# Products of queries and projection matrix: from one unrounded product per head to three products of rounded operands in halves of the array, with the queries and the matrix split beforehand

## What is computed

```python
def features(data, proj, is_query):             # data: q or k, 12 heads, 625 x 64
    dash = einsum('bhnd,md->bhnm', data * 64 ** -0.25, proj)   # proj: 266 x 64
    diag = sum(data ** 2, -1) * 0.5 * 64 ** -0.5
    stab = max(dash, -1) if is_query else max(dash)            # per row, or over everything
    return 266 ** -0.5 * (exp(dash - diag - stab) + 1e-4)
q1, k1 = features(q, P, True), features(k, P, False)
kv = einsum('bhnm,bhnd->bhmd', k1, v)
out = einsum('bhnm,bhmd->bhnd', q1, kv) / einsum('bhnm,bhm->bhn', q1, sum(k1, 2))
```

## Time and profile of the kernel before

| | |
|---|---|
| median of 3 runs | 1195.68 us (1194.62 to 1196.69) |
| the profiled execution, its own time | 1196.4 us |
| its span in the trace | 1194.7 us |
| mean granted clock of TensorE | 0.985 of full speed |
| TensorE busy | 1142.5 us, 96% |
| VectorE / ScalarE / GpSimd busy | 762.3 / 657.6 / 450.2 us |
| float32 feature products of the queries (L1704) | 120 instructions, from 204.1 to 285.8 us |

### The profile page before, as it was taken

One profiled execution on the slowest core, in us unless ns is written; L12 is line 12 of the kernel. 1 busy time (PEld: TensorE's weight loads), 2 busy tenths in 40 slices (PEclk: granted clock), 3 DMA queues, 4 the chain that ended last, 5 costly groups with the idle time before them and its releaser, 6 DMA issues.

```text
span 1194.7 us, 20786 instructions
## 1 busy us (share of the span) xinstructions
PE 1142.5 (96%) x6492; PEld 1008.1 (84%) x6493; DVE 762.3 (64%) x1226; ACT 657.6 (55%) x1040; POOL 450.2 (38%) x340
## 2 busy tenths in 40 slices
PE   6989999999999999999999999999999999999985
PEld 5989998888665778989999888888889989998874
DVE  7881454365587466526956865647775896666883
ACT  3222575165400154347686685757876878386963
POOL 1188888788811000542122231203223542122511
PEclk9989999999989999999999999999999999999998
DMA  9030003340300330166687565565785959377933
GB/s 312 18 89 3 2 2 82 113 140 3 87 9 18 103 118 13 28 182 222 212 305 259 211 233 187 176 224 187 285 295 203 367 188 335 83 274 286 351 118 97
DMA packets 63088, 191.71 MB, mean 160 GB/s; under 512 B 14315, under 2 KB 15382, under 8 KB 63044
## 3 DMA queue, kind: packets, MB, share of 16 engines
q1 hardware_dynamic: 51316, 172.86, 39.6%
q0 software_dynamic: 11728, 18.27, 8.9%
HBM read 178.74 MB, written 15.09 MB: 162 GB/s over the span
## 4 chain that ended last, share of the span: by engine, by line
PE 78%; DVE 9%; issue 4%; ACT 4%; DMA 3%; POOL 1%; ACTq 0%; SPq 0%; DVEq 0%; POOLq 0%
PE banks L1939 25%; PE banks L1923 24%; PE banks L1689 3%; PE banks L1704 3%; PE banks L1837 3%; PE banks L1859 3%; PE banks L1672 3%; PE banks L1907 2%; PE banks L1761 2%; PE banks L1739 2%; PE banks L1911 2%; ACT kfeat L1432 2%; DMA out<-ysb,sidx 2%; PE banks L1900 1%; DVE oh L962 1%
## 5 line engine op out<-in xcount | busy, mean ns | idle before, releaser
L730 POOL DMA_INDIRECT edge_dram<-epair,eslot x165 | 219.6, 1331 | 98.9 <-issue 98.9
L520 ACT ACTIVATE w2hi<-w2raw 128x1536 fp32r<-128x1536 f32 x96 | 139.2, 1483 | 95.3 <-DMA w2raw<-in_L_ffn_fc_w 83.7
L794 POOL DMA_INDIRECT out<-ysb,sidx x27 | 84.9, 3143 | 264.8 <-issue 231.0
L533 DVE TENSOR_TENSOR w2lo<-w2raw,w2hi 128x1536 fp32r<-128x1536 f32 x96 | 164.4, 1754 | 25.9 <-ACT w2hi L520 23.8
L1939 PE MATMUL banks<-w2hi,hthi 128*128 128x384 f32 x624 | 161.7, 340 | 0.1
L1939 PE MATMUL banks<-w2hi,htlo 128*128 128x384 f32 x624 | 159.2, 335 | 0.0
L1939 PE MATMUL banks<-w2lo,hthi 128*128 128x384 f32 x624 | 158.9, 335 | 0.0
L520 ACT ACTIVATE w1hi<-w1raw 128x1536 fp32r<-128x1536 f32 x96 | 137.8, 1498 | 27.2 <-DMA w1raw<-in_L_ffn_fc_w 25.9
L1923 PE MATMUL banks<-w1hi,xthi 128*128 128x512 f32 x486 | 139.7, 396 | 2.7 <-POOL w1lo L533 2.7
L533 DVE TENSOR_TENSOR w1lo<-w1raw,w1hi 128x1536 fp32r<-128x1536 f32 x80 | 141.6, 1834 | 0.1
L1923 PE MATMUL banks<-w1lo,xthi 128*128 128x512 f32 x486 | 136.8, 390 | 0.0
(11 more groups left out here) (347 smaller groups left out, 1866.2 us busy)
## 6 DMA issues: line engine op xcount, KB each, us to landing
w1raw<-in_L_ffn_fc_w SPq DMA_DIRECT2D x96, 768.0 KB
w2raw<-in_L_ffn_fc_w SPq DMA_DIRECT2D x96, 768.0 KB, 6.4
xs<-in_x SPq DMA_DIRECT2D x10, 336.0 KB
edge_dram<-epair,eslot POOLq DMA_INDIRECT x165
wg<-in_L_gnn_W SPq DMA_DIRECT2D x1, 2304.0 KB, 12.5
wv<-in_L_mix_W_qkv SPq DMA_DIRECT2D x1, 2304.0 KB, 13.9
wk<-in_L_mix_W_qkv SPq DMA_DIRECT2D x1, 2304.0 KB, 17.8
wq<-in_L_mix_W_qkv SPq DMA_DIRECT2D x1, 2304.0 KB, 12.0
```

The costliest lines, as they stand in the source:

```text
L520: act.activation(unit(w2hi if second else w1hi, second, u), unit(w2raw if second else w1raw, second, u), ACT.Copy).then_inc(w2_hi if secon ...
L533: eng.tensor_tensor(unit(w2lo if second else w1lo, second, u), unit(w2raw if second else w1raw, second, u), unit(w2hi if second else w1hi, ...
L730: pool.indirect_dma_start(out=edge_dram, out_offset=bass.IndirectOffsetOnAxis(ap=eslot[:, k:k + 1], axis=0), in_=epair[:, k, :].bitcast(I3 ...
L794: pool.indirect_dma_start(out=out, out_offset=bass.IndirectOffsetOnAxis(ap=sidx[:, 0:1], axis=0), in_=ysb[:, :], in_offset=None, bounds_ch ...
```

## The change

Queries and matrix are split as other operands are. ScalarE copies `projt` into `projhi` and each tile's queries into `qhi`; the first two of these stand ahead of the last two key exponentials, behind a wait for all squares, the other four after them. VectorE makes `projlo` after the last key features, in place of `projt`, and `qlo` in place of `qt`: tile 0 right after it, the others between the key-value copies. TensorE waits for `projlo` ahead of the key tails. `query_pair` replaces two calls of `project`: it waits for the banks of both heads and for the tile's low part, and then makes three rounds (high x high, high x low, low x high) of one product per head. The keys' products (`ddk`) stay as they are. `projhi` lies where `xs` has its fifth row tile, so that tile's second load moves behind the last transposes.

```diff
--- before.py
+++ after.py
@@ -163,6 +163,8 @@
         hs = at("hs", 89088, [TP, NT, D])
         xn2 = at("xn2", 73728, [TP, NT, D])
         qt = at("qt", 104192, [128, C, N])
+        qlo = at("qlo", 104192, [128, C, N], F32R)
+        qhi = at("qhi", 88832, [128, NT, C, TP], F32R)
         xn2t = at("xn2t", 104448, [128, 2, C, TP])
         kt = at("kt", 119296, [128, C, N])
         q1 = [at("q1a", 119296, [TP, H, M]), at("q1b", 132128, [TP, H, M])]
@@ -274,6 +276,8 @@
         eslot = at("eslot", s0 + 1344, [TP, ET], U32)
         bsplit = small("bsplit", [128, F + D], BF16)
         projt = at("projt", s0, [128, M])
+        projlo = at("projlo", s0, [128, M], F32R)
+        projhi = at("projhi", 198560, [128, M], F32R)
         nbias = at("nbias", s0 + 1472, [TP, 4, 60])
         lnst = at("lnst", s0 + 1472, [TP, NT, 2, 6])
         lnmv = at("lnmv", s0 + 1728, [TP, NT, 2])
@@ -433,7 +437,7 @@
 
         half_hi, half_lo, vones_ok, sq_ok, sq_used, kmax_ok, kbias_ok, kexp_ok, k1_ok = sems(
             "half_hi half_lo vones_ok sq_ok sq_used kmax_ok kbias_ok kexp_ok k1_ok")
-        qbias_ok, q1_ok, q1t_used, bsplit_zero = sems("qbias_ok q1_ok q1t_used bsplit_zero")
+        q_high, q_low, proj_high, proj_low, qbias_ok, q1_ok, q1t_used, bsplit_zero = sems("q_high q_low proj_high proj_low qbias_ok q1_ok q1t_used bsplit_zero")
         gate_pad, shared_rows, shared_ok, xt_zero = sems("gate_pad shared_rows shared_ok xt_zero")
 
         x1_ok, xn2_ok, sc_ok, ex_ok, member_ok, slots_ok, btab_ok = sems(
@@ -606,10 +610,13 @@
             sp.dma_start(bias1_dram.rearrange("g e (j c) -> (e j) g c", j=8), bias_s[:, :, 0:F // 8]).then_inc(st_bias, 16)
             sp.dma_start(bias2_dram.rearrange("g e (j c) -> (e j) g c", j=8), bias_s[:, :, F // 8:]).then_inc(st_bias, 16)
 
-            done(sp, ("sqq", 0))
-            for i in range(NT):
+            def rows_again(i):
                 for a, b in ((0, 112), (112, TP)):
                     sp.dma_start(xs[a:b, i, :], x[TP * i + a:TP * i + b, :]).then_inc(ld_x[i], 16)
+
+            done(sp, ("sqq", 0))
+            for i in range(NT - 1):
+                rows_again(i)
             sp.dma_start(wp[:, :, :], w_proj.rearrange("(c p) n -> p c n", c=C)).then_inc(ld_wp, 16)
 
             fc1_units = fc1_w.rearrange("e (c p) n -> e p c n", c=C)
@@ -630,6 +637,7 @@
             sp.dma_start(bias2[:, 0, :], row(gnn_b).broadcast_to([TP, D])).then_inc(ld_bias, 16)
             sp.dma_start(bias2[:, 1, :], row(b_proj).broadcast_to([TP, D])).then_inc(ld_bias, 16)
             done(sp, ("q1t", 4, H // 2 - 1))
+            rows_again(NT - 1)
             sp.wait_ge(st_offs, 16)
             sp.dma_start(offs[:, :], row(region_dram)[:, 0:ET_TILES]).then_inc(ld_offs, 16)
             for u in range(3):
@@ -1082,6 +1090,18 @@
                 dve.tensor_scalar(q1tail[:, i % 2, heads, :], q1[i % 2][:, heads, MAIN:M], FEAT_EPS, ratio,
                                   ALU.add, ALU.mult).then_inc(q1_ok, 1)
 
+            def query_low(i):
+
+                dve.wait_ge(q_high, i + 1)
+                t = slice(TP * i, TP * i + TP)
+                dve.tensor_tensor(qlo[:, :, t], qt[:, :, t], qhi[:, i, :, :].bitcast(F32), ALU.subtract).then_inc(q_low, 1)
+
+            dve.wait_ge(proj_high, 1)
+            done(dve, ("ddk", NT - 1, H - 2))
+            done(dve, ("ddk", NT - 1, H - 1))
+            dve.tensor_tensor(projlo[:, :], projt[:, :], projhi[:, :].bitcast(F32), ALU.subtract).then_inc(proj_low, 1)
+            dve.wait_ge(sq_ok, 2 * C)
+            query_low(0)
             squares_to(("sqq", 0), 1)
             taken(dve, ("sqq", 0))
             for g in range(2):
@@ -1095,6 +1115,8 @@
                     emptied(dve.tensor_copy(kv[:, h, :, :], ps[:, 0:2 * (HD + 1)].rearrange("p (m d) -> p m d", m=2)), ("kv", h))
                     if h % 2:
                         q_bias(0, h // 2)
+                    if h in (1, 3, 5, 9):
+                        query_low((h + 1) // 2 if h < 9 else NT - 1)
                     if h == 7:
                         q_features(0, 0)
 
@@ -1447,7 +1469,19 @@
             for n in range(2, 10):
                 exp_keys(7 * n - 12, 7 * n - 5)
                 take_columns("q", (n + 2) // 2, (n % 2,))
+            act.wait_ge(sq_ok, 2 * C)
+            act.activation(projhi[:, :], projt[:, :], ACT.Copy).then_inc(proj_high, 1)
+            for o in range(C):
+                for s in range(2):
+                    taken(act, ("q", o, s))
+
+            def query_high(i):
+                act.activation(qhi[:, i, :, :], qt[:, :, TP * i:TP * i + TP], ACT.Copy).then_inc(q_high, 1)
+
+            query_high(0)
             exp_keys(58, H * NT)
+            for i in range(1, NT):
+                query_high(i)
 
             def q_exp(i, p):
                 for h in (2 * p, 2 * p + 1):
@@ -1717,6 +1751,18 @@
                     filled(pe.matmul(ps[0:TP, 0:TP], kmax[0:TP, 0:1].broadcast_to([TP, TP]), ident[0:TP, 0:TP],
                                      start=True, stop=True), ("kmx", 0))
 
+            def query_pair(i, r):
+
+                parts = [(fill(pe, ("ddq", i, h)), HD * (h % 2), h) for h in (2 * r, 2 * r + 1)]
+                pe.wait_ge(q_low, i + 1)
+                for k, (of, w) in enumerate(((qhi, projhi), (qhi, projlo), (qlo, projhi))):
+                    for ps, a, h in parts:
+                        stationary = qlo[a:a + HD, r, TP * i:TP * i + TP] if of is qlo else qhi[a:a + HD, i, r, :]
+                        last = pe.matmul(ps[0:TP, 0:M], stationary, w[a:a + HD, :], start=k == 0, stop=k == 2)
+                        if k == 2:
+                            filled(last, ("ddq", i, h))
+
+            pe.wait_ge(proj_low, 1)
             pe.wait_ge(vones_ok, 1)
             for s in range(2):
                 taken(pe, ("v", NT - 1, s))
@@ -1740,8 +1786,7 @@
                                              vext[:, i, h, :], start=i == 0, stop=i == NT - 1)
                     filled(last, ("kv", h))
                     if h % 2:
-                        project("ddq", qt, 0, h - 1)
-                        project("ddq", qt, 0, h)
+                        query_pair(0, h // 2)
 
 
             def turn_pair(i, p):
@@ -1782,8 +1827,7 @@
                         filled(pe.transpose(ps[0:TAILS, 0:TP], q1tail[:, i % 2, :, :].rearrange("p h m -> p (h m)"),
                                             ident[0:TP, 0:TP]), ("tail", i))
                     for r in AHEAD[p] if i + 1 < NT else ():
-                        project("ddq", qt, i + 1, 2 * r)
-                        project("ddq", qt, i + 1, 2 * r + 1)
+                        query_pair(i + 1, r)
                     attend(i, p)
```

## The result

The changed kernel takes **1206.99 us** (median of 4 runs, 1206.45 to 1209.77), the one before 1195.96 in the same comparison (1194.62 to 1196.69): ratio 1.0101, 95% interval 1.0085 to 1.0117. It is slower, as forecast, but by 11.0 us where I had 5.6, and above the range of 1198.6 to 1205.5. Its profiled execution took 1206.46 us.

What follows compares the result with a forecast made beforehand. TensorE, busy 96% of the span, was taken as the bound, with no slack at the seam behind the key exponentials. +5.25 + 1.75 - 0.46 - 0.9 = +5.6 us gave 1201.3 us, range 1198.6 to 1205.5.

Steps and rivals of the forecast that it cites:

- Seam, (a) to (d): Between query-column products and key-value products: waits for the splits add 5.25 us, the lower clock after TensorE's stop 1.75.
- the place of the wait: TensorE waits for the matrix's low part ahead of all key tails, so eight early tail instructions come behind it: 2.6 us.
- (a): At the seam ScalarE makes two high parts before the last two key exponentials, so the last features come 2.25 us later.
- (b): At the seam VectorE then makes the matrix's low part, 0.44 us, done at 199.8.
- (d): TensorE's idle stop at the seam lowers its clock for 3.5 us of work, half lost: +1.75 us, bounds 0 and 3.4.
- Pairs in tile 0: Six pairs between tile 0's key-value products, where TensorE is the pace, gain 0.46 us in all.
- in a stream: Pairs following each other take 0.375 us each, 0.073 less than now; three pairs take 1.34 us instead of 1.62.
- Rival (1): In the pairs the array's halves take turns, 0.75 us a pair: in all +13.6 us, 1209.3; chance 0.10.
- rival (2): Weight loads set the pairs' pace, 0.54 us a pair: in all +9.0 us, 1204.7; chance 0.12.
- Loop: The 24 pairs in the loop over tiles gain 0.22 us per tile, 0.9 in four; bounds 0 and 2.8.
- rival (4): Not slower: 1.2 GHz stretches near 239, 330 and 346 us vanish and the new stop is free, 1194.5; chance 0.04.
- Moved: Row tile 4's second load goes later at no cost, under 2 us if late; a later TensorE is passed on in full.

Runs made afterwards that it cites:

- filler_10: Changed kernel with GpSimd held behind VectorE's five additions, plus ten useless products ahead of TensorE's wait for the matrix's low part: 1198.52 us, ratio 1.0027.
- filler_late_6: Changed kernel, GpSimd held back, TensorE's low-part wait moved behind the half sums, six useless products ahead of the last key tail: 1202.25 us, ratio 1.0053.
- pool_wait: Changed kernel with GpSimd waiting for VectorE's five additions before splitting its part of the first expert: 1201.03 us, ratio 1.0050.
- unrounded: Changed kernel with all splits and waits, but one unrounded product per head, from the low parts alone: 1207.11 us, ratio 1.0104.
- the fourth: Fourth set of follow-up runs, with the changed kernel and the one holding GpSimd back side by side; the kernel before took 1194.37 us in it.
- the second set: Set of follow-up runs in which every kernel was slower by some 20 us; the kernel before took 1216.44 us, the changed one 1229.57.
- meet: Changed kernel with VectorE's fifth addition waiting until GpSimd has issued its last scatter, so that addition and difference run side by side: 1207.59 us, ratio 1.0115.
- meet_not: Changed kernel with VectorE's fifth addition waiting for GpSimd's last scatter, and GpSimd's difference then waiting for the addition: 1205.83 us, ratio 1.0114.
- after_five: Changed kernel unaltered, run again beside the one with GpSimd held back: 1206.33 us, ratio 1.0084.
- pool_five: Changed kernel with GpSimd's difference held behind VectorE's fifth addition, run again beside the unaltered one: 1205.54 us, ratio 1.0081.
- early_split: Changed kernel with the matrix split before the query products, queries behind the last exponentials, and TensorE's low-part wait behind the half sums: 1195.21 us, ratio 1.0007.
- after_third: Changed kernel unaltered, run once more in the third set: 1201.94 us, ratio 1.0065.
- late_wait: Changed kernel with only TensorE's wait for the matrix's low part moved from ahead of the key tails to behind the half sums: 1223.48 us, ratio 1.0233.
- the first set: First set of follow-up runs, which asked which part of the changed kernel costs the time; the kernel before took 1195.01 us in it.
- after_beside: Changed kernel unaltered, traced in the same set as the kernel before: 1206.33 us, ratio 1.0108.
- early_rest: Changed kernel with the seam's split made early and three VectorE weight differences moved behind the graph convolution's first sums: 1193.03 us, ratio 1.0000.

## Why the prediction was right, and where it was wrong

The account is that of the two profiled executions, +10.0 us against the predicted +5.6. The direction was right and the size was not.

- **Seam, (a) to (d): right.** 13.46 - 6.33 = 7.13 us, predicted 7.00. The links hold singly: the high parts 0.42 and 0.83 (0.40, 0.80), the low part 0.42 (0.44), the clock 1.9 to 2.1 in the tails, 1.7 net by filler_10 (1.75), the place of the wait 2.5 by filler_late_6 (2.6). That the sum fits to 0.1 is partly luck: the first tail behind the wait came 2.5 us later where (a) and (b) said 2.7, and the clock took a little more than (d).
- **Pairs in tile 0: right; in a stream: mis-sized.** kv is 0.40 us shorter (0.46), and the two halves run side by side. Rival (1) is out. Eighteen instructions in a stream last 1.59 us (272.87 to 274.46), not 1.34, close to the 1.6 at which I would have given rival (2) its way: a pair follows the other by 0.48 us, where I had 0.375. The spacing isn't even, though. The rounds between 273.10 and 273.59 are 0.12 us apart, a product every 0.06; the first round takes 0.1 longer, and the third pair begins 0.1 late and has a long first round again, for a reason that no record shows. The Trainium skill (TensorE: Matmul & The Clock Gate, section "Back-to-back issue gap") has about 81 ns for a load and a product at 128 columns. Over the whole stream the trace comes near it (0.078 us each), inside the middle rounds it is faster (0.06), and the measurement decides. So three pairs in a stream gain 0.02 us (1.54 to 1.52), and a lone pair 0.08.
- **Loop: right by the pairs, wrong in the sum.** 0.22 per tile was forecast, and pool_wait beside unrounded shows 0.19 and 0.30. Yet both pairs of traces, before and changed, show 0.3 to 0.4 more for the loop, where I had 0.9 less. Tile 0 gained 0.7 to 0.8 (the kernel before has a stretch at 1.2 GHz near 239 us there, one of rival (4)'s, and the changed one doesn't); later tiles lost up to 0.8 each. In the six traces with complete records and a clock of 0.97 or more at the loop's start the same code takes 70.1 to 71.4 us. What lengthens it in other sets stays open, and so does the clock lost in tile 0 in the fourth. Outside the second set the kernel before never took more than 1198.0 us, while the changed one ranged from 1198.2 to 1214.9: it is less steady.
- **Moved: the step that failed.** "A later TensorE is thus passed on in full" took the work of the other engines behind the attention as moving along with TensorE. GpSimd's scatters don't: outside the second set they end between 319 and 325 us, whether the loop over tiles ends at 306 or at 335. Arriving eight us later, VectorE's fifth addition fell upon the difference of weights that GpSimd does behind them, and the stage grew from 22.17 to 26.49, +4.3 us, where I had nothing. This is shown by meet and meet_not by stage (3.9), by after_five against pool_five by stage (3.6), and early_split, after_third and the kernel before, whose additions are over earlier, don't have it. A TensorE that comes later still doesn't escape: in late_wait and after_five GpSimd's difference was held by ScalarE, moved along, and the first addition met it. As a total only the first set speaks for it (pool_wait at 1201.0), and there the loop has a share; in the fourth the totals scatter by more than the meeting costs. How many of the executions without a trace had the meeting isn't known.
- The rest, 864.6 to 862.2 us, is 2.4 shorter, and 1.0 us of delay was there ahead of the seam. Executions of code that is the same there differ as much (861.8 to 864.9; outside the second set the last product of query columns starts between 192.3 and 194.8). Yet both traces of the kernel before have one of the longest rests, and all four of the changed kernel outside the second set a short one, by 2.1 to 3.0 us. The difference arises in the experts, more than 146 us behind the first one-hot product; whether the change has to do with it stays open.
- +1.0 + 7.1 - 0.4 + 0.4 + 4.3 - 2.4 = +10.0. Take the meeting out of the measured 1206.99 and 1202.7 is left, within the range, but with the unexplained -2.4 in it. The price isn't one number either: in four other sets the changed kernel's ratio was 1.0142, 1.0065, 1.0084 and 1.0108.

## What to carry to other kernels

A delay is not passed on unchanged past the point at which another engine works at its own pace: look at what that engine will be doing when the delayed work arrives, above all VectorE's additions and differences in SBUF beside GpSimd's. Splits that precede a product belong into time that some engine has, not ahead of the last step of a chain: moved, they cost nothing here. And a stop of TensorE is to be priced with the clock behind it, read from the clock column for the order at hand: some 4 us of work at the lower level here, 33 after a shorter stop in another order. Last, a difference of 1 to 4 us should be read by stages, with a pair of kernels that differ in that one thing: the totals here varied by more.

## What the runs showed of the hardware

- A wait of 3.3 us cost more than one of 6.3: in late_wait the clock stayed at 0.50 from 202 to 235 us while TensorE was busy throughout.
- VectorE's addition, recorded 0.30 us ahead of GpSimd's difference, still stood through it: 4.56 us for 0.95 (4.55 twice more, in after_beside and meet). Where GpSimd's was recorded 0.76 us ahead, the addition took 4.09 to 4.11.
- Rounded products in the two halves of the array stream side by side in either order of the list, every 0.12 us for 266 columns in the middle of a stream; with its slower rounds a stream of three pairs has one pair every 0.48 us.
- GpSimd's scatters of edges take 1.2 us, and 1.4 to 1.8 beside VectorE's additions and differences in SBUF (2.69 once, in the kernel before); without three of these, in early_rest, the last ones take 1.19.
